# Causal mask of the row maximum added in PSUM by TensorE, and one plain maximum over two heads

## The reference, cut to what matters

```python
scores = jnp.einsum('bhqd,bhkd->bhqk', q, k) * scale
mask = jnp.where(kpos > qpos, jnp.float32(-jnp.inf), jnp.float32(0.0))
attn = jax.nn.softmax(scores + mask[None, None], axis=-1)
out = jnp.einsum('bhqk,bhkd->bhqd', attn, v)
```

## Time and profile before

| | |
|---|---|
| median of 3 runs | 2275.24 us (2273.57 to 2276.34) |
| span of the profiled execution | 2275.4 us |
| TensorE busy | 2066.5 us, 91% |
| VectorE busy | 1781.7 us, 78% |
| ScalarE busy | 1432.0 us, 63% |
| mean granted TensorE clock | 0.956 of full |

### The profile page before, as it was taken

One profiled execution on the slowest core, in us unless ns is written; L12 is line 12 of the kernel. 1 busy time (PEld: TensorE's weight loads), 2 busy tenths in 40 slices (PEclk: granted clock), 3 DMA queues, 4 the chain that ended last, 5 costly groups with the idle time before them and its releaser, 6 DMA issues. The chain is left out here.

```text
span 2275.4 us, 39173 instructions
## 1 busy us (share of the span) xinstructions
PE 2066.5 (91%) x11796; PEld 826.6 (36%) x11796; DVE 1781.7 (78%) x2710; ACT 1432.0 (63%) x2695; POOL 278.8 (12%) x274
## 2 busy tenths in 40 slices
PE   6756899999989999998999999989999998768998
PEld 4431333332223322232332332233332233546887
DVE  6978788887658888864888887658888863896886
ACT  3440567776866766777666777867767776224554
POOL 5650000000000000000000000000000000562442
PEclk9875899999999999999999999999999999898999
DMA  4555100000120000012100000120000013302231
GB/s 149 157 125 103 37 9 9 9 9 1 55 68 16 9 9 6 5 29 67 37 9 9 8 9 9 57 59 16 9 9 9 1 39 121 108 10 82 98 115 47
DMA packets 91334, 98.44 MB, mean 43 GB/s; under 512 B 10848, under 2 KB 85104, under 8 KB 91120
## 3 DMA queue, kind: packets, MB, share of 16 engines
q1 hardware_dynamic: 89032, 94.22, 14.4%
q10 hardware_dynamic: 2100, 1.72, 0.6%
HBM read 67.65 MB, written 16.78 MB: 37 GB/s over the span
## 5 line engine op out<-in xcount | busy, mean ns | idle before, releaser
L978 ACT ACTIVATE prob<-banks 128x512 f32<-128x512 f32 (+3 forms) x2304 | 1177.6, 562 | 465.4 <-PE banks L918 299.6
L1017 DVE TENSOR_REDUCE mx<-banks 128x2 f32<-128x1024 f32 x920 | 1080.3, 1220 | 226.7 <-PE banks L842 225.5
L918 PE MATMUL banks<-q_aug,k_aug 108*128 108x512 bf16 (+3 forms) x2304 | 711.6, 367 | 16.2 <-issue 13.4
L842 PE MATMUL banks<-k_aug,q_aug 96*128 96x512 bf16 (+1 forms) x2016 | 566.6, 375 | 86.0 <-DMA q_aug<-parts_scratch 28.9
L886 PE MATMUL banks<-prob,v_cur 128*17 128x512 f32 (+3 forms) x4608 | 566.5, 564 | 0.1
L918 PEld LDWEIGHTS banks<-q_aug,k_aug 108*128 108x128 bf16 x2304 | 222.2, 97 | 666.9 <-issue 309.9
L1022 DVE CUSTOM_DVE_ANT_0 banks<-banks,mask_sb 128x128 f32<-128x128 f32 (+3 forms) x560 | 260.2, 521 | 88.9 <-PE banks L842 79.3
L842 PEld LDWEIGHTS banks<-k_aug,q_aug 96*128 96x128 bf16 x2016 | 170.2, 98 | 314.6 <-issue 161.8
L1058 POOL CAST nm_p<-nm 128x16 bf16<-128x16 f32 x35 | 7.4, 212 | 1715.4 <-DVE nm L1031 1715.4
L886 PEld LDWEIGHTS banks<-prob,v_cur 128*17 128x17 f32 x4608 | 76.4, 95 | 201.1 <-issue 157.6
L923 PE MATMUL banks<-later_k,id_b 128*128 128x128 bf16 x512 | 107.8, 227 | 0.0
(11 more groups left out here) (120 smaller groups left out, 1643.9 us busy)
## 6 DMA issues: line engine op xcount, KB each, us to landing
w_s<-in_w SPq DMA_DIRECT2D x16, 1024.0 KB, 5.5
parts_scratch<-p SPq DMA_DIRECT2D x96, 128.0 KB, 2.4
xs<-in_x SPq DMA_DIRECT2D x16, 512.0 KB, 3.6
k_aug<-parts_scratch SPq DMA_DIRECT2D x40, 192.0 KB, 2.7
q_aug<-parts_scratch SPq DMA_DIRECT2D x35, 192.0 KB, 2.8
v_cur<-v_all SPq DMA_DIRECT2D x40, 136.0 KB, 2.0
k_aug<-parts_scratch SPq DMA_DIRECT2D x40, 128.0 KB, 2.5
q_aug<-parts_scratch SPq DMA_DIRECT2D x35, 128.0 KB, 3.1
```

What stands on the lines that cost most here:

```text
L842: mm = nc.tensor.matmul(slot[:, jj * CW:jj * CW + width], q_aug[0:KROWS, c % QRING, j, t * P:(t + 1) * P], keys[0:KROWS, j, kc * CW:kc * C ...
L918: mm = nc.tensor.matmul(score[u % SBANKS][:, q0:CW], k_aug[0:KROWS + MROWS, j, kb * P:(kb + 1) * P], q_aug[0:KROWS + MROWS, c % QRING, j, ...
L978: nc.scalar.activation(prob[:, s % PROBS, j, q0:CW], score[u % SBANKS][:, q0:CW], ACT.Exp, scale=float(HD) ** -0.5).then_inc(exp_done[u % ...
L1017: nc.vector.tensor_reduce(mx[:, c % QRING, t, 2 * pair:2 * pair + 2, kc], slot.rearrange("p (j s) -> p j s", j=2), AX_X, ALU.max).then_inc ...
```

## The change

A diag unit gets its causal mask from TensorE. After each of the two score matmuls a second one of 128 columns adds `later_k` transposed onto the last 128 columns of the block in PSUM, in the way that the main stream's diagonal is masked. VectorE then takes one `tensor_reduce` over both heads, of the unit's width, as for a full unit. The SBUF mask, its load and the semaphore between the two custom instructions go; `later_k` is loaded at the place of the mask, and TensorE waits for it before the head part. The planner's estimate of a diag unit changes in both numbers.

```diff
@@ side_cost
     if kind == "diag":
-        return 2 * (t + 1) * P * PE_COLUMN, 2 * (75 + (t + 1) * P * 1.04)
+        return 2 * (t + 2) * P * PE_COLUMN, 100 + 2 * (t + 1) * P * 1.02
@@ attend_block
-    mask = sb("mask_sb", [P, CW])
@@ SP
                 if r == 0:
-                    sp.dma_start(mask[:, :], a["mask"]).then_inc(mask_in, 16)
-            sp.dma_start(later_k[:, :], a["later"]).then_inc(consts_in, 16)
+                    sp.dma_start(later_k[:, :], a["later"]).then_inc(mask_in, 16)
             sp.dma_start(k_aug[KROWS:KROWS + MROWS, :, :], a["lastones"]).then_inc(consts_in, 16)
@@ TensorE, side_unit
                         mm = nc.tensor.matmul(slot[:, jj * CW:jj * CW + width],
                                               q_aug[0:KROWS, c % QRING, j, t * P:(t + 1) * P],
                                               keys[0:KROWS, j, kc * CW:kc * CW + width], start=True, stop=True)
+                        if kind == "diag":
+                            mm = nc.tensor.matmul(slot[:, jj * CW + t * P:jj * CW + width], later_k[:, :], id_b[:, :],
+                                                  start=False, stop=True, skip_group_check=True)
@@ TensorE
             pe.wait_ge(id_cast, 1)
+            pe.wait_ge(mask_in, 16)
...
-            pe.wait_ge(consts_in, 32)
+            pe.wait_ge(consts_in, 16)
@@ VectorE
-            dve.wait_ge(mask_in, 16)
...
-                if kind == "diag":
-                    alone(dve, passed_dve)
-                if kind == "full":
+                if kind in ("full", "diag"):
+                    width = CW if kind == "full" else (t + 1) * P
                     nc.vector.tensor_reduce(mx[:, c % QRING, t, 2 * pair:2 * pair + 2, kc],
-                                            slot.rearrange("p (j s) -> p j s", j=2), AX_X, ALU.max).then_inc(free, 1)
-                elif kind == "diag":
-                    width = (t + 1) * P
-                    for jj in range(2):
-                        ins = nc.vector.tensor_tensor_reduce(
-                            slot[:, jj * CW:jj * CW + width], slot[:, jj * CW:jj * CW + width], mask[:, CW - width:CW],
-                            1.0, NEG, ALU.add, ALU.max, mx[:, c % QRING, t, 2 * pair + jj, kc:kc + 1])
-                        ins.then_inc(max_done if jj == 0 else free, 1)
-                    if t == TILES - 1 and pair == 1:
+                                            slot.rearrange("p (j s) -> p j s", j=2)[:, :, 0:width], AX_X, ALU.max)\
+                        .then_inc(free, 1)
+                    if kind == "diag" and t == TILES - 1 and pair == 1:
```

More of the change, by code:

```diff
@@ L195, in build @@
 def build(nc, x, wqk, wvT, woT, lnsb, attnT, attnb, w1, b1, w2, b2, nextT, nextb, cvec, wmod,
-          rope, ident, mask, later, lastones, out):
+          rope, ident, later, lastones, out):
     parts = nc.dram_tensor("parts_scratch", [PARTS, 2, HD // 2, 2 * JH, QUADS, S], BF16, kind="Internal").ap()
@@ L220, in build @@
             x=x, wqk=wqk, wvT=wvT, woT=woT, cvec=cvec, wmod=wmod, rope=rope, ident=ident, parts=parts,
-            id_f=id_f, mod_bc=mod_bc, mod_col=mod_col, wo_g=wo_g, att_o=att_o, mask=mask, later=later, lastones=lastones))
+            id_f=id_f, mod_bc=mod_bc, mod_col=mod_col, wo_g=wo_g, att_o=att_o, later=later, lastones=lastones))
         feed(nc, sem, bank, dict(
@@ L715, in attend_block @@
     nm_done, cut_done = sem("nm_done"), sem("cut_done")
-    max_done, linv_done = sem("max_done"), sem("linv_done")
+    linv_done = sem("linv_done")
     def exp_count(g, u):
@@ L1676, in constants @@
 def constants():
-    mask = np.zeros((P, CW), np.float32)
     q, k = np.arange(P)[:, None], np.arange(P)[None, :]
-    mask[:, CW - P:] = np.where(k > q, np.float32(-1e38), np.float32(0))
     later = np.where(q > k, np.float32(-1e30), np.float32(0)).astype(mybir.dt.np(BF16))
@@ L1683, in constants @@
         last[PARTS * j:PARTS * (j + 1), j, :] = 1
-    return {"rope": rope_table(), "ident": np.eye(P, dtype=np.float32), "mask": mask, "later": later, "lastones": last}
+    return {"rope": rope_table(), "ident": np.eye(P, dtype=np.float32), "later": later, "lastones": last}
 def kernel(**inputs):
```

## The result

The changed kernel runs in 2294.55 us (median, 2292.89 to 2295.78) against 2274.4 us: ratio 1.0092, 95% interval 1.0079 to 1.0104. It is 20 us slower, over three times the forecast of +6, and 2.6 us outside the range.

A forecast was written before the change was run, and what follows sets the result against it. TensorE was taken to bound the 1680 us loop. Diag units +7, planner -1 and head 0 gave +6 us on the profiled 2275.4 us: 2281 us, range 2270 to 2292.

The forecast's parts named there:

- The planner: Order of side units: new diag-unit estimates, nearer the traced times, spread full units a little; -1 us, between -8 and +5.
- The walk through the diag units: Loop's diag units, followed chunk by chunk: 29.7 us of mask matmuls added, 22.5 us of TensorE pause gone, +7 us.
- The rival "faster": Diag stretches: masked pauses (24.8 us) and half the plain ones (12 us) go; -7 us, 2268 us; chance 14%.
- the pauses go altogether: Loop: TensorE's 24.8 us of pauses behind masked maxima all go, nothing more; +4 us, 2277 to 2279 us; chance 20%.
- The head: Head part and loads: +0.8 us from diag units, -0.5 us from an earlier first maximum; sum about 0.

The follow-up runs named there:

- old_plan_pad16: The changed kernel with the planner's old cost of a diag unit and 16 empty semaphore instructions ahead of TensorE's head part; 2270.89 us, ratio 0.9984.
- after_pad16: The changed kernel with 16 empty semaphore instructions ahead of TensorE's head part; 2286.87 us, ratio 1.0058.
- mix_pad16: As old_plan_pad16, but loop diag units of chunks 0 to 2 keep two masked custom maxima, and `alone` precedes every diag maximum; 2273.85 us, ratio 0.9999.
- relief_only: The kernel before, order and TensorE work unchanged, with one plain unmasked maximum per diag unit, no `alone`, exponential scale 0.01; 2245.38 us, ratio 0.9873.
- before_pad97: The kernel before with 97 empty semaphore instructions ahead of TensorE's head part, so its loop begins where the changed kernel's does; 2290.68 us, ratio 1.0081.

## Why the prediction was wrong

The direction was right and the range missed by 2.6 us. Two steps failed and cost some 25 us against the forecast; that the miss is only 14 us is luck, as the relief of VectorE was worth some 10 us more than forecast in the loop, and the head gave 2.6 us.

**The planner: the failed step.** "I take -1 us for this", with bounds of -8 and +5. It was +16 us (old_plan_pad16 to after_pad16), +15 without the padding, +21 in the kernel before. The prediction reasoned that an estimate nearer to the traced one must give an order with fewer pauses, and took +5 us as the worst from "32 places" moved by 0.15 us. The planner's own output for the two kernels differs in the places of 182 of the 304 side units. `side_cost` is a knob as much as a measurement: the planner knows nothing of the 0.2 us between a score's last column and the start of its maximum (0.41 us from the start of a 512-column score, of which 0.215 is streaming), nor of the time between a freed slot and the next matmul. In the loop the d-d waits moved from 5.1 to 14.1 us and the turn units' from 5.6 to 7.9; plain units waited 9 us less behind plain units and 5.5 us more behind turns, norms and diag units. In all the pauses grew by 13.7 us.

**The loop turn: a term left out.** +8.8 us. The prediction listed what each wait costs and left out the 13.4 us of "issue" ahead of a pass's first score, since nothing of the change seemed to touch it. 97 more instructions ahead of the loop did.

**The walk through the diag units: mis-sized.** Forecast: 29.7 us added, 22.5 us of pause gone, +7. On the old order and with the turn as it was, measured: loop 1682.6 against 1685.5, -2.9 us. That is 29.7 added and 32.5 of pause gone (120.7 to 88.2): side 24.9, turn units 2.7, short pauses before main scores and the turns of the loop the rest. Of the d-d pauses 20 of 25 us went. The price of the matmul held: 0.058 us. The Trainium skill, "TensorE: Matmul & The Clock Gate", section "Back-to-back issue gap", which the prediction cites, has about 81 ns; the trace does not bear it out for this stream. Too low was what the relief buys, and the part of it that the prediction put at nothing is the semaphore instruction ahead of each diag maximum: 0.15 us of relief was taken for a unit, and it is some 0.28 us where VectorE waits for scores. With that instruction back, mix_pad16 has 5.7 us more pause in the stretches of chunks 3 to 7 alone. By chunk, before against old_plan_pad16, some 25 us of pause went in chunks 3 to 7, where the walk had 20, and 7.6 us in chunks 0 to 2, where it had some 3.

The rival "faster" had the amount, more than 30 us of pause taken back, but not the reason: plain units behind plain units waited 36.5 us before and 36.2 after. Nearly all came from diag units' own waits, which is the rival "the pauses go altogether" and more. Had only the two engines' work changed, the result would have been old_plan_pad16's -4 us, which is within what counts as the same.

**The head: right in kind.** "About 0", with +0.8 and -0.5 as its parts: it is -2.6 us. The first maximum began at 173.02 (173.2 forecast); more of VectorE's relief showed than the half that was taken. relief_only, without mask matmuls, shortens the head by 3.0 us, so they cost little there.

So the 20 us are: -2.9 us of work against relief on the loop's old order, +14.5 us of order (loops of old_plan_pad16 and after_pad16), +9.5 us for the loop's place in the code (after_pad16 and the changed kernel; 9.2 of it at the turns) and -2.6 us in the head. That makes 18.5 against the 18.6 between the two traces' spans; the medians differ by 20.1. That order and turn add up was tested by old_plan_pad16, whose 2271 us was worked out before it ran. What stays open is which placement rule makes the old order good; only that six tried orders differ by up to 16 us is shown.

## What to carry to other kernels

When a change also edits the numbers of a planner, run those numbers alone first, and count how many places they move: here they cost more than everything else. Count the empty semaphore instructions that a change takes away or leaves, in the experiments too: one between a wait and the work delays the work. An engine that is idle a quarter of the time can still pay more than the busy one, where two engines hand two buffers to and fro: judge its work by the pauses of the other, short ones included, which are read from starts and not from printed idle times. Look at every wait at a loop's turn: instructions added ahead of the loop lengthened it here, with its own code unchanged.

## What the runs showed of the hardware

- The turn of a long loop on TensorE takes 4 to 5 us, or 7 to 8 us, for nothing but where the loop begins in the code: 13.0 and 22.2 us for three turns of the same loop, 16 instructions apart. The difference is a second wait of 3.0 to 3.8 us, between the loop's second and third instruction in all twelve slow turns.
- A matmul of 128 columns in a stream where each has its own weights takes 0.06 us from start to start, with 96 rows and 128 rows in turn.
- A plain maximum in PSUM takes 0.422 us for 256 elements and 1.220 for 1024: 1.04 ns an element and 0.156 us fixed. Two custom maxima of half the width each took 0.12 to 0.15 us longer, from the first start to the last end.
- A semaphore instruction on TensorE that does nothing else takes 0.15 us (97 of them from 164.8 us on in before_pad97, first matmul at 179.8). One on VectorE between its wait and a maximum makes the maximum start 0.11 us later (0.37 us after the last matmul's start in mix_pad16, 0.26 in old_plan_pad16).
